# Last node group with 312 columns in feed-forward and experts, and four VectorE instructions fewer in each chunk's chain of maxima

## The reference, cut to what matters

```python
x = x + _L0_gnn_ref(_layernorm(x), edges, ...)   # attention over edges, then a feed-forward part
x = x + _L0_ffn_ref(_layernorm(x)[None], ...)[0] # 8 experts, softmax router
# in the first: per edge and head, with a segment maximum over the edges of one destination
alpha = jnp.sum(q[dst] * k[src], axis=-1) / sqrt(D)
m = jax.ops.segment_max(alpha, dst, num_segments=n)
ex = jnp.exp(alpha - m[dst])
out = segment_sum(ex * v[src], dst) / segment_sum(ex, dst) + x @ Wskip
h = _layernorm(x + out)
h = _layernorm(h + gelu(h @ W1 + b1) @ W2 + b2)
# in the second, for each expert e, three products of 256x256 with relu after two of them
y = relu(bn(relu(bn(x @ W1[e])) @ W2[e])) @ Wo[e];  out += softmax(mean(x) @ Wr)[e] * y
```

## Time and profile before

| | |
|---|---|
| median of 3 runs | 1502.57 us (1501.42 to 1509.48) |
| profiled execution, its own time | 1504.69 us, mean granted PE clock 0.933 |
| its span, first to last instruction | 1502.9 us |
| busy share of the span | PE 83%, DVE 72%, POOL 62%, ACT 54% |
| gathers | 464, 466.5 us busy |
| DMA | mean 117 GB/s over the span |

### The profile page before, as it was taken

How to read it: one execution, slowest core, us unless ns; L and a number is a source line. 1 busy time by engine, 2 the same in 40 slices (tenths; PEclk the granted TensorE clock), 3 DMA queues, 4 the chain that set the end, 5 groups by cost and what they waited for, 6 DMA issues and landing times. The chain is left out here.

```text
span 1502.9 us, 24128 instructions
## 1 busy us (share of the span) xinstructions
PE 1247.5 (83%) x6835; PEld 966.9 (64%) x6835; DVE 1078.1 (72%) x2557; ACT 810.3 (54%) x2534; POOL 930.9 (62%) x883
## 2 busy tenths in 40 slices
PE   7988776677767677667657889999999999999998
PEld 3444454454445444444445578889898899999998
DVE  7647877777777787777868779886766665656655
ACT  1356766556666766566657654565543344444443
POOL 3365566656666665666665556866765477667765
PEclk9999879888898898998988999999999999999999
DMA  7477766666666666666665120101000000000002
GB/s 222 162 218 210 224 192 192 178 180 185 199 186 199 178 199 174 201 172 197 184 180 166 31 75 29 52 27 40 9 15 22 1 22 15 8 22 15 1 12 76
DMA packets 74072, 175.40 MB, mean 117 GB/s; under 512 B 11500, under 2 KB 36651, under 8 KB 73945
## 3 DMA queue, kind: packets, MB, share of 16 engines
q0 software_dynamic: 37632, 124.28, 29.6%
q1 hardware_dynamic: 34641, 48.25, 9.6%
q10 hardware_dynamic: 1672, 1.33, 0.3%
HBM read 159.91 MB, written 13.91 MB: 116 GB/s over the span
## 5 line engine op out<-in xcount | busy, mean ns | idle before, releaser
L690 POOL DMA_INDIRECT ring<-kv_rows,idx x464 | 466.5, 1005 | 296.4 <-issue 116.6
L764 ACT ACTIVATE ring<-ring 128x64 f32<-128x64 f32 x1800 | 442.1, 336 | 17.2 <-issue 16.1
L1287 POOL TENSOR_TENSOR wm<-k_gf,wm 128x512 fp32r<-128x512 f32 (+1 forms) x224 | 264.0, 1181 | 147.1 <-DVE wm L1786 147.1
L1386 ACT ACTIVATE k_gf<-psF,k_scT 128x512 f32<-128x512 f32 (+1 forms) x224 | 164.0, 733 | 258.3 <-PE psF L1557 258.3
L1786 DVE CAST wm<-k_gf 128x512 fp32r<-128x512 f32 (+1 forms) x224 | 168.8, 758 | 158.7 <-ACT k_gf L1386 157.0
L810 PE MATMUL psA<-ring,oh 128*128 128x260 f32 x912 | 274.1, 429 | 7.5 <-DVE k_acc L1016 7.1
L784 PE MATMUL psQ<-k_q,ohT 128*128 x1392 | 225.3, 304 | 58.7 <-issue 58.2
L982 DVE TENSOR_TENSOR prod<-psQ,ring 128x512 f32<-128x512 f32 x232 | 157.4, 678 | 89.5 <-remote 59.9
L784 PEld LDWEIGHTS psQ<-k_q,ohT 128*128 128x128 bf16 x1392 | 131.9, 105 | 115.7 <-issue 86.0
L810 PEld LDWEIGHTS psA<-ring,oh 128*128 128x128 f32 x912 | 178.0, 217 | 36.5 <-issue 8.5
L1022 DVE TENSOR_REDUCE alpha<-prod 128x8 f32<-128x512 f32 x232 | 155.6, 671 | 0.2
(11 more groups left out here) (284 smaller groups left out, 2671.9 us busy)
## 6 DMA issues: line engine op xcount, KB each, us to landing
ohT<-step_destinations SPq DMA_DIRECT2D x29, 512.0 KB
ring<-kv_rows,idx POOLq DMA_INDIRECT x464
kv_rows<-kvst SPq DMA_DIRECT2D x25, 260.0 KB, 2.4
we<-in_L_ffn_W SPq DMA_DIRECT2D x16, 256.0 KB, 2.8
residual<-qst SPq DMA_DIRECT2D x25, 128.0 KB
xs<-in_x SPq DMA_DIRECT2D x2, 1024.0 KB, 8.8
resin<-residual SPq DMA_DIRECT2D x4, 512.0 KB
we<-in_L_ffn_Wo SPq DMA_DIRECT2D x8, 256.0 KB, 2.7
```

The lines of the kernel that those rows point to most:

```text
L690: nc.gpsimd.indirect_dma_start(out=ring[:, LT * (j % CP) + k, j // CP:j // CP + 2, :].rearrange("p t e -> p (t e)"), out_offset=None, in_= ...
L764: last = nc.scalar.activation(row[:, 0:D], row[:, 0:D], ACT.Copy, scale=row[:, D:HW_])
L1287: nc.gpsimd.tensor_tensor(low[:, i % 2, m, 0:w], gf[:, n % 4, 0:w], high[:, i % 2, m, 0:w], ALU.subtract).then_inc(s_gl, 1)
L1386: nc.scalar.activation(gf[:, n % 4, 0:cols(g)], ps, ACT.Relu, bias=bias, scale=scale).then_inc(s_ev, 1)
```

## The change

In **attend**, four DVE instructions of each chunk's chain go. The copies `cin` and `bin_` of a psR column go, and the scans F2 and Gm take their initial value from psR itself. The wait for PE that stood ahead of each copy stands ahead of the scan now, one place later. The copy of `carry` into column 0 of `tails` goes, and PE writes that column with a product of its own, ahead of the one that writes the others. The one-hot row oh0 goes. A row of ones, set once, takes its place, so that PE's product hands fx to every row, and `fac` is the maximum of it and noh. ScalarE's program has no instruction more or fewer. In **tail**, the last group's three blocks have 128, 128 and 56 columns (RC, 53 rounded up to 8) where they had 128 each.

```diff
+RC = -(-REST // 8) * 8
-(V_ALPHA, V_F1, V_CARRY, V_INH, V_CIN, V_F2, V_B1, V_BACK, V_IV, V_FD, V_FMIN, V_OH0, V_NEXT, V_BIN, V_G,
- V_DIFF, V_FAC) = range(1, 18)
-NV = 17
+(V_ALPHA, V_F1, V_CARRY, V_INH, V_F2, V_B1, V_BACK, V_IV, V_FD, V_FMIN, V_G, V_DIFF, V_FAC) = range(1, 14)
+NV = 13
...
                 if jj == 1:
                     pe.wait_ge(s_mv, NV * m + V_F1)
+                    if m:
+                        nc.tensor.matmul(tails[:, :, 0], one[0:1, 0:1], carry[:, :, W], start=True, stop=True)
                     nc.tensor.matmul(tails[:, :, 1:W + 1], F1[:, P - 1:P], ident[0:R, 0:R], start=True, stop=True).then_inc(s_mp, 1)
...
-                    nc.tensor.matmul(psM[0:BP, 400:400 + H], oh0[:, :], fx[:, :], start=True, stop=True).then_inc(s_mp, 1)
+                    nc.tensor.matmul(psM[0:BP, 400:400 + H], orow[:, :], fx[:, :], start=True, stop=True).then_inc(s_mp, 1)
...
+            nc.vector.memset(orow[:, :], 1.0)
...
-                if at == (3, 0):
+                if at == (3, 1):
                     dve.wait_ge(s_mp, mp + T_CARRY)
-                    nc.vector.tensor_copy(cin[:, :], psR[0:R, 128:129]).then_inc(s_mv, 1)
-                if at == (3, 1):
-                    seen(V_CIN)
-                    nc.vector.tensor_tensor_scan(out=F2[:, :], data0=nrow[:, 0:P], data1=psM[0:R, 0:P], initial=cin[:, 0:1],
+                    nc.vector.tensor_tensor_scan(out=F2[:, :], data0=nrow[:, 0:P], data1=psM[0:R, 0:P], initial=psR[0:R, 128:129],
                                                  op0=ALU.add, op1=ALU.max).then_inc(s_mv, 1)
...
                     nc.vector.tensor_scalar(fm[:, :], fd[:, :], 0.0, None, ALU.min).then_inc(s_mv, 1)
-                    nc.vector.tensor_scalar(oh0[:, :], iotaF[0:1, 0:BP], dstR[0:1, bass.ds(W * m, 1)], None,
-                                            ALU.is_equal).then_inc(s_mv, 1)
+                if at == (5, 1):
                     dve.wait_ge(s_mp, mp + T_IV)
-                    nc.vector.tensor_copy(tails[:, :, 0], carry[:, :, W]).then_inc(s_mv, 1)
-                    nc.vector.tensor_copy(bin_[:, :], psR[0:R, 384:385]).then_inc(s_mv, 1)
-                if at == (5, 1):
-                    seen(V_BIN)
                     nc.vector.tensor_tensor_scan(out=Gm[:, ::-1], data0=psM[0:R, P + 1:2 * P + 1][:, ::-1], data1=F2[:, ::-1],
-                                                 initial=bin_[:, 0:1], op0=ALU.add, op1=ALU.max).then_inc(s_mv, 1)
+                                                 initial=psR[0:R, 384:385], op0=ALU.add, op1=ALU.max).then_inc(s_mv, 1)
...
         def cols(g):
-            return CH[g] * BP
+            return CH[g] * BP if g < NC - 1 else (CH[g] - 1) * BP + RC
+
+        def rows_in(g, u):
+            return RC if g == NC - 1 and u == CH[g] - 1 else BP
...
                     for u in pair:
-                        out = ps[:, (u % 2) * HID:(u % 2 + 1) * HID]
-                        at = slice(u * BP, (u + 1) * BP)
+                        n = rows_in(g, u)
+                        out = ps[0:n, (u % 2) * HID:(u % 2 + 1) * HID]
+                        at = slice(u * BP, u * BP + n)
                         for k in range(KC):
                             nc.tensor.matmul(out, h2h[:, i % 2, k, at], lo[:, k, :], start=(k == 0), stop=False)
```

More of the change, by code:

```diff
@@ L560, in attend @@
         oh = sb("oh", [P, NO, LT, BP])
-        oh0 = sb("oh0", [1, BP])
+        orow = sb("orow", [1, BP])
         prod = sb("prod", [P, 2, LT * HID])
@@ L570, in attend @@
         Gm = sb("Gm", [R, P])
-        cin = sb("cin", [R, 1])
-        bin_ = sb("bin_", [R, 1])
         carry = sb("carry", [1, H, W + 1])
@@ L966, in maximum @@
                     nc.vector.tensor_scalar(fac[:, :], psM[0:BP, 400:400 + H], noh[:, at_noh:at_noh + 1], None,
-                                            ALU.add).then_inc(s_mv, 1)
+                                            ALU.max).then_inc(s_mv, 1)
             def at(i, j, fresh):
@@ L1482, in router @@
                 for u in range(size(g)):
-                    t = (first(g) + u) * BP
+                    t, n = (first(g) + u) * BP, rows_in(g, u)
                     for k in range(KC):
-                        nc.tensor.matmul(psT[:, 2 * NE * u:2 * NE * (u + 1)], xh[:, k, t:t + BP], wrs[:, k, :],
+                        nc.tensor.matmul(psT[0:n, 2 * NE * u:2 * NE * (u + 1)], xh[:, k, t:t + n], wrs[:, k, :],
                                          start=(k == 0), stop=False)
                     for k in range(KC):
-                        last = nc.tensor.matmul(psT[:, 2 * NE * u:2 * NE * u + NE], xl[:, k, t:t + BP], wrs[:, k, 0:NE],
+                        last = nc.tensor.matmul(psT[0:n, 2 * NE * u:2 * NE * u + NE], xl[:, k, t:t + n], wrs[:, k, 0:NE],
                                                 start=False, stop=(k == KC - 1))
```

## The result

The changed kernel takes 1518.11 us (median of 20 runs, 1503.73 to 1526.54) where the kernel before takes 1501.68 (20 runs, 1494.26 to 1509.48): ratio 1.0104, 95% interval 1.008 to 1.0128. It is 1% slower. The forecast was 1490 us, and the time lies outside the range (1481 to 1498). All ratios here come from the fast runs alone, without the few that lay over 1.5% above the fastest of their kernel, so they can differ by some tenths of a per cent from the quotient of the medians. The profiled execution of the changed kernel took 1505.06 us (span 1503.2), one of its shortest, so its rows understate the loss.

The account below looks back on a forecast made before the run. PE was taken to bound the experts; in attend, DVE and POOL were nearly saturated between silent spells. Profiled 1504.7 less 7.1 (tail) and 5.5 (attend) gave 1492.1, or 1490.0 us as a median; range 1481 to 1498.

Parts of the forecast that it names:

- The spells: Attend: silent stretches where DVE and POOL see PE's signals late; faster DVE means 2% fewer, gaining 2.8 us.
- third rival: Attend: denser DVE work makes spells more frequent, about 2.2 us each; slower from nine more, 1508.5 us; chance 0.05.
- POOL's standing: Attend: POOL's 128 us of standing over 416 gathers should fall by 3 to 6 us.
- a phase: Attend: if spells depend on something shifted, such as PE's chain against the gathers, tens of us either way; no chance given.
- the moved waits: Attend, DVE: two waits placed behind the one-hot matrix cover 0.33 us of work each time; 2.7 us taken, 6.6 at most.
- The count of standing pieces: Attend, POOL: 128 us of standing read as some 60 to 70 pieces, two to three in each of 26 chunks.
- DVE's side: Attend: removed copies and oh0 save 0.39 us a chunk, 11.3 us over 29 chunks; 17.9 with moved waits.
- second rival: Attend: nothing arrives, POOL's 20.9 us a chunk and the spells take all; 1495.5 us; chance 0.17.
- The scans' reading of PSUM: Attend, DVE: scans taking their start value from psR cost nothing, at most 3.5 us.
- PE's extra product: Attend: the product writing the tails column is covered by 1.1 us; without cover up to 29 x 0.2 = 5.8 us.
- The tail: Last group's 312 columns: experts 5.8, feed-forward 1.0 and the very end 0.3, together 7.1 us gained.
- fourth rival: Tail: matmul spacing stays near 173 ns at 312 columns, so the tail gives only 0.3 us; 1496.8 us; chance 0.03.

Follow-up runs that it names:

- e2: The changed kernel's four attend edits alone, with the tail of the kernel before: 1526.37 us, ratio 1.0193 to the kernel before.
- e3: Changed kernel with column 0 of tails again copied by DVE, in the new place, and no extra PE product: 1522.77 us, ratio 1.0116 to the kernel before.
- e1: Kernel before with only the tail's 312-column last group, its attend chain untouched: 1486.83 us against 1499.31, ratio 0.9928.
- g3: Second run of the kernel before with only the tail's 312-column last group, where spells are: 1489.4 us, ratio 0.9937.
- g2: Changed kernel plus four unused DVE instructions of the old sizes in the old places, where spells are: 1517.11 us, ratio 1.0119 to the kernel before.
- i1: Changed kernel with DVE's two waits for PE back in their old substeps, scans still reading PSUM: 1507.26 us against 1494.22 for the kernel before, ratio 1.0091.
- g1: Changed kernel with ACT making the next chunk's indices one step earlier, where spells are: 1481.76 us against 1498.79 for the kernel before, ratio 0.9887.
- f1: The changed kernel itself run again, on a chip without spells: 1352.14 us against 1358.91 for the kernel before, ratio 0.9945.

## Why the prediction was wrong, step by step

**The spells.** The prediction took them as a fixed tax that thins out a little with a faster DVE, gain 2.8 us, and in its third rival made the harm depend on more spells, nine from where it is slower. That step failed: attend, which was to gain 5.5 us, lost 12.1 between the two profiles and 27 to 29 in e2. The number of the spells stayed (47 and 48), and most still cost 2.1 us. What changed is their place, and the price has two levels: about 2.1 us inside a chunk and 3.9 at its boundary. Between the profiles of before and after, the pauses elsewhere fell from 83 to 70 us and those at the boundary rose from 29 to 59; the difference of 17 us is the 14 us by which 184 steps grew, with a little shared by other waits. POOL's standing was to fall by 3 to 6 us from 128, and rose: its 412 gathers in the changed kernel have 262.3 us of gaps, less 412 x 0.30 that is 139. The row for it was in the earlier trace rows: 40.9 us of waiting for `idx`. I read it as one more name of the same spell; I should have asked why that wait reached 6.2 us in the list of waits when others ended at 2.7. The last sentence of the prediction named a phase as what would overthrow it, but with "tens of us either way" for a price and with no chance.

Three numbers of the prediction were wrong in themselves. The third rival's 1508.5 us takes 7.1 and 5.5 off twice: 1502.6 + 31 - 12.6 is 1521. That the measured 1518.11 lies near it is luck, since no more spells came. And the moved waits would cover the one-hot matrix, which lasts 0.40 us by the earlier trace rows; the 0.33 us used for it are the price of oh0 and the copies. The count of standing pieces was too high: 60 to 70 in 26 chunks were read out of the sum, two to three in each, and by my count it is 47 in 23, two in each.

**DVE's side.** 11.3 us of less work was right as work: over the 184 steps, 23 of 29 chunks, DVE is busy 448.1 us before and 438.6 after, 9.5 us less (9.0 of the 11.3 belong to these). Nothing of it arrives. With the boundary's price gone the new chain takes 580.3 us for these steps and the old one 577.6, DVE's busy time is 439.6 and 448.0, its idle time 140.7 and 129.6: what is saved comes back as idle time. That is the outcome of the second rival, nothing arrives in attend. Without spells it is so too, since POOL's issuing is the bound there. The moved waits (2.7 us) gave nothing that could be seen.

**The scans' reading of PSUM** costs 8 ns each, 58 x 8 = 0.5 us; taking nothing for it was right.

**PE's extra product** was covered, as e3 shows: without it the time doesn't fall.

**The tail** was forecast at 7.1 us and measured at 10.9 in e1's profile (669.2 us from the last product to the end before, 658.3 in e1), at 9 to 11 by the ratios of e1 and g3. The mechanism holds. PE in the changed kernel's last expert, and one of POOL's halves:
```profile
1493.73 0.46 PE L1553 MATMUL psF<-wm,gT 128*128 128x312 f32 x2
1494.03 0.31 PE L1550 MATMUL psF<-wm,gT 128*128 128x312 f32 x1
...
1494.60 0.45 PE L1553 MATMUL psF<-wm,gT 128*128 128x312 f32 x2
...
1495.27 0.85 POOL L1283 TENSOR_TENSOR wm<-k_gf,wm 128x312 fp32r<-128x312 f32 x1 [2.10 <-DVE wm L1784]
```
Six matmuls lie between 1493.73 and 1494.60, 145 ns each (143 forecast), and the low half takes 0.85 us instead of 1.02. By the row above, spacing follows the columns and not the flatter rule of the Trainium skill that the prediction weighed ("TensorE: Matmul & The Clock Gate", "Back-to-back issue gap"): the fourth rival is dead. The experts' stretch, from the first product of the first expert to the end, fell from 451.4 to 442.7 us, by 8.7 and not 6.1. Some 1.7 us of that is no gain of the change: the profile of before has a dip of PE's granted clock to half (1.2 GHz) in it that the changed kernel's lacks. (Both have 0.93 on the mean between 1075 and 1100 us.) The window from 1151.6 to 1155 us of the kernel before:
```profile
1151.60:1155.00 3.40, 3.40 (x11) 3.17 (x10) 0.63 (x2) 1.34 (x2) 1.00 (x1) 0.50 0.20 69
```
The clock there is 0.50 of full speed, and what takes 3.4 us here takes 1.7 elsewhere: products of 384 columns start 0.32 us apart in it and 0.17 us apart just before. The rest of the surplus, 2 to 3 us, lies between the last product and the experts, where 1.0 was forecast; I haven't divided it further.

**What stays open.** Why the spells of the kernels without the two copies settle at the boundary. DVE's shorter work alone (g2), the place of the waits alone (i1) and PE's product (e3) are each excluded as the single cause. The rival that is left is the starting value read from PSUM. It is the one edit that all six kernels with 15 pauses and more share, and no kernel has it with the old waits and the old amount of work. The wait's place and the work together haven't been tried either. Nor has the row of ones by itself where spells are. What the spell itself is, the traces don't tell; a mark of it stands in the last section.

## What to carry to other kernels

Where stalls come with a period of their own, ask what each engine needs next at the place where the stall may fall, and price the dearest place, not the mean one: here one ACT instruction that stood behind a wait doubled the price of every stall at a chunk's boundary, and moving it by a step took 2.1% off the changed kernel and 0.7% off the old chain. Make small work that another engine waits for at the boundary ahead of the waits, not behind them. And before taking work from an engine, check who sets the pace between its stalls; DVE, idle for a quarter of the stretch, had 11 us less to do, and nothing of that arrived.

## What the runs showed of the hardware

Two kinds of chips ran the same program: the kernel before took 1494 to 1502 us on some and 1359 to 1361 on others, and the mean clock granted to PE in it was 0.93 to 0.95 and 0.98. On the first, POOL pauses about once per 8 indirect gathers, 47 to 50 times in 369 gathers in every kernel but one, with a lead of five steps as with eight; g1 has 54. In the kernel before, in 32 of the 47 pauses the first engine that had stood over 0.7 us goes on 0.8 to 1.6 us after POOL's last gather ended. On the others 410 gathers go out with never more than 0.3 us between them.

The traces of the two kinds differ in one more thing. This is the page's line on the landing of the gathers, in the kernel before and in f1:
```profile
ring<-kv_rows,idx POOLq DMA_INDIRECT x464
```
```profile
ring<-kv_rows,idx POOLq DMA_INDIRECT x464, 3.9
```
The first has no time to landing because most of the signals are not in the trace. The 464 gathers send 16 each, 7,424 in all. In f1 all are recorded, and the signals that PE, ACT and DVE give in each step lie 0.01 us behind their instructions. In the kernel before 2,730 of the gathers' signals are recorded, and of PE's 232 signals for psQ 187; in the tail, where no gathers run, none of PE's 280 signals for psF is missing. Every kernel with spells has this (2,721 to 2,918 of 7,424), and none without (7,419 to 7,424). So a spell goes with a thinning of all signals while gathers run. Whether signals are held up, merged, or only their records lost, the trace doesn't say. It also means that in rows from chips with spells "remote", or the releaser that is named, can stand for a gather whose signal wasn't recorded.

The two kinds of chips are 9% of the time apart, nine times what the change is worth, and that turned the change's sign. What makes the chips differ, no run here tells.
